# Four stacked graph layers on one core: how the edge keys are made, which branch body comes first, and where the last turned copies stand

## Time and profile before

| | |
|---|---|
| median of 3 runs | 1550.4 us (1550.18 to 1551.41) |
| the profiled execution | 1550.59 us |
| its span, first to last instruction | 1548.6 us |
| TensorE (PE) busy | 1516.2 us, 98% |
| VectorE (DVE) busy | 881.2 us, 57% |
| ScalarE (ACT) busy | 751.6 us, 49% |
| GpSimd (POOL) busy | 189.9 us, 12% |
| mean granted TensorE clock | 0.997 |
| bytes by DMA | 231.88 MB, mean 150 GB/s |

### The profile page before, as it was taken

How to read it: one execution, slowest core, us unless ns; L and a number is a source line. 1 busy time by engine, 2 the same in 40 slices (tenths; PEclk the granted TensorE clock), 3 DMA queues, 4 the chain that set the end, 5 groups by cost and what they waited for, 6 DMA issues and landing times.

```text
span 1548.6 us, 19194 instructions
## 1 busy us (share of the span) xinstructions
PE 1516.2 (98%) x6956; PEld 1218.0 (79%) x6956; DVE 881.2 (57%) x1403; ACT 751.6 (49%) x1358; POOL 189.9 (12%) x315
## 2 busy tenths in 40 slices
PE   5989999999999999999999999999999999999997
PEld 4877877778887887788877777888888778877775
DVE  7877888887736343322433244567598356434346
ACT  5666766767734333333332234345597236533232
POOL 1101021234300000000000000112143013100003
PEclk9999999999999999999999999999999999999999
DMA  5333143324774433434353424564466248535345
GB/s 175 121 110 132 42 167 128 112 75 158 253 259 174 132 136 112 166 106 138 100 172 125 156 68 145 189 233 168 143 184 194 87 149 294 189 129 171 93 126 179
DMA packets 103328, 231.88 MB, mean 150 GB/s; under 512 B 23167, under 2 KB 26102, under 8 KB 103226
## 3 DMA queue, kind: packets, MB, share of 16 engines
q1 hardware_dynamic: 90126, 191.66, 38.8%
q10 hardware_dynamic: 13100, 38.86, 6.5%
HBM read 171.11 MB, written 59.37 MB: 149 GB/s over the span
## 4 chain that ended last, share of the span: by engine, by line
PE 90%; DVE 5%; ACT 3%; issue 1%; DMA 0%; POOL 0%; DVEq 0%; SPq 0%; POOLq 0%; ACTq 0%
PE bank L974 16%; PE bank L836 15%; PE bank L838 15%; PE bank L837 15%; PE bank L985 9%; PE bank L978 7%; PE bank L976 7%; PE bank L1038 2%; ACT Tt L1119 2%; PE bank L906 1%; DVE Tt L1423 1%; PE bank L874 1%; DVE oK L1698 1%; ACT Mh L1101 0%; ACT Zh L1153 0%
## 5 line engine op out<-in xcount | busy, mean ns | idle before, releaser
L836 PE MATMUL bank<-wh,xh 128*125 128x512 f32 x1032 | 415.9, 403 | 0.0
L837 PE MATMUL bank<-wl,xh 128*125 128x512 f32 x1040 | 410.8, 395 | 0.0
L838 PE MATMUL bank<-wh,xl 128*125 128x512 f32 x1040 | 410.0, 394 | 0.0
L974 PE MATMUL bank<-Zh,Mh 125*125 125x512 f32 x1000 | 399.4, 399 | 0.0
L1397 DVE TENSOR_TENSOR xl<-xs,xh 128x1000 fp32r<-128x1000 f32 x130 | 155.5, 1198 | 291.6 <-ACT xh L1084 291.3
L1084 ACT CAST xh<-xs 128x1000 fp32r<-128x1000 f32 x130 | 132.9, 1026 | 304.2 <-PE bank L838 292.8
L985 PE MATMUL bank<-Zl,Mh 125*125 125x512 f32 x600 | 236.6, 394 | 0.0
L838 PEld LDWEIGHTS bank<-wh,xl 128*125 128x125 f32 x1040 | 193.3, 186 | 49.0
L837 PEld LDWEIGHTS bank<-wl,xh 128*125 128x125 f32 x1040 | 193.4, 186 | 44.5
L836 PEld LDWEIGHTS bank<-wh,xh 128*125 128x125 f32 x1032 | 191.4, 185 | 44.6
L974 PEld LDWEIGHTS bank<-Zh,Mh 125*125 125x125 f32 x1000 | 185.4, 185 | 44.7
(11 more groups left out here) (173 smaller groups left out, 1812.2 us busy)
## 6 DMA issues: line engine op xcount, KB each, us to landing
xs<-xT_d SPq DMA_DIRECT2D x80, 500.0 KB, 3.5
Ar<-a_d SPq DMA_DIRECT2D x100, 312.5 KB, 3.3
xs<-hT_d SPq DMA_DIRECT2D x40, 500.0 KB, 3.5
x_d<-XO ACTq DMA_DIRECT2D x30, 512.0 KB, 5.1
R<-x_d SPq DMA_DIRECT2D x60, 256.0 KB, 4.3
xT_d<-XT ACTq DMA_DIRECT2D x30, 500.0 KB, 3.8
ws<-in_W SPq DMA_DIRECT2D x30, 256.0 KB, 3.6
Tt<-m_d SPq DMA_DIRECT2D x10, 625.0 KB, 5.0
```

Of the source, the lines that this page charges most:

```text
L836: te.matmul(o, xh[i % 2][:, k, :], wh[s][:], start=(k == 0), stop=False)
L837: te.matmul(o, xh[i % 2][:, k, :], wl[s][:], start=False, stop=False)
L838: m = te.matmul(o, xl[i % 2][:, k, :], wh[s][:], start=False, stop=(k == 7))
L974: te.matmul(o, Mh[i][:, s, :], zh, start=(n == 0), stop=False)
```

## The change

- `WIN` becomes 37 nodes for every chunk, centred on round((125 c + 62) / 17), no longer clipped. The table `win` and its load go. The centre `mid` is made on the chip from `iot`, which now starts at -180 (`ZERO` = 180 is where its value is 0).
- `ef`, `wt` and the two comparisons go. `off` = dst - mid is taken straight from the integers; one instruction takes the largest square of it, and the flag compares that with 18 squared. hi is rounded in two steps instead of three, lo16 is made in one step, kb = 10 off + hi. The general body makes `lo` and `key` for itself.
- TensorE's branch is written out: the counting body comes first, then the general one. The counting body ends with a jump over the general body. A hint for this jump is marked 30 chunks ahead.
- The whole copy into `A16` is a function of its own, `counts_whole`. For t = 9 it runs after counts_turned(9) and the first tanh, which now comes after counts_turned(9). VectorE runs degrees(5, 10) before times.

```diff
-MARGIN = 250
+REACH = 18
+HINT = 30
+ZERO = NT * REACH
+WHOLE = 12582912.0
-WIN = [(max(0, (T * c - MARGIN) // PER), min(N - 1, (T * c + T - 1 + MARGIN) // PER)) for c in range(NC)]
+WIN = [(round((T * c + T // 2) / PER) - REACH, round((T * c + T // 2) / PER) + REACH) for c in range(NC)]
...
-            sy.dma_start(wn_[:], win.rearrange("p (a c) -> p a c", a=3)).then_inc(d_edge, 16)
...
-                with te.If(v > 0):
+                te.br_cond(v < 1, on_true="pe_chunks", on_false="pe_general")
+                with nc.body("pe_chunks", valid_engines=[te.engine]):
+                    for c in range(NC):
+                        if c == NC - HINT:
+                            hint = te.mark_branch_hint_location()
+                        chunk(c)
...
+                    te.br("pe_counted").branch_hint(hint)
+                after, q.seen = q.seen, before
+                with nc.body("pe_general", valid_engines=[te.engine]):
                     te.sem_inc(gP, 1)
...
+                    te.br("pe_counted")
+                nc.switch_bb("pe_counted")
...
+                if t < NT - 1:
+                    counts_whole(t)
+
+            def counts_whole(t):
+                q.wait_ge(s_ev, 3 * t + 3)
                 if t >= 2:
                     q.wait_ge(d_a[t % 2], 16 * (t // 2))
-                q.wait_ge(s_ev, 3 * t + 3)
                 q.wait_ge(s_pad, 2)
                 ac.copy(A16[t % 2], Af[t % 2][:]).then_inc(s_a16, 1)
...
-                if t == NT - 1:
-                    tanh(J0[0], blocks_of(J0[0], EARLY))
                 counts_turned(t)
...
+            tanh(J0[0], blocks_of(J0[0], EARLY))
+            counts_whole(NT - 1)
             first_part(J0[0], EARLY)
...
-                q.wait_ge(d_edge, 48)
-                chain("v", ve.tensor_copy(ef[:], ei[:]))
-                mine()
-                chain("v", ve.tensor_tensor(wt[:, 0, :], wn_[:, 0, :], ef[:, 1, :], ALU.subtract))
-                chain("v", ve.tensor_tensor(wt[:, 1, :], ef[:, 1, :], wn_[:, 1, :], ALU.subtract))
-                mine()
-                chain("v", ve.reduce_max(sm[0:T, 0:1], wt[:].rearrange("p a c -> p (a c)"), AXX))
-                mine()
-                ve.tensor_scalar(sm[0:T, 1:2], sm[0:T, 0:1], 0.0, None, ALU.is_gt).then_inc(s_flag, 1)
+                q.wait_ge(s_pool0, 1)
+                chain("v", ve.tensor_scalar(mid[:], iot[:, ZERO:ZERO + NC], float(T) / PER, float(T // 2) / PER, ALU.mult,
+                                            ALU.add))
+                mine()
+                chain("v", ve.tensor_scalar(mid[:], mid[:], WHOLE, -WHOLE, ALU.add, ALU.add))
+                mine()
+                q.wait_ge(d_edge, 32)
+                chain("v", ve.tensor_tensor(off[:], ei[:, 1, :], mid[:], ALU.subtract))
+                mine()
+                chain("v", ve.tensor_tensor_reduce(out=key[:], in0=off[:], in1=off[:], scale=1.0, scalar=0.0, op0=ALU.mult,
+                                                   op1=ALU.max, accum_out=sm[0:T, 0:1]))
+                mine()
+                ve.tensor_scalar(sm[0:T, 1:2], sm[0:T, 0:1], REACH * REACH + 0.5, None, ALU.is_gt).then_inc(s_flag, 1)
...
-                chain("v", ve.scalar_tensor_tensor(lo[:], hi[:], -float(T), ef[:, 0, :], ALU.mult, ALU.add))
-                chain("v", ve.scalar_tensor_tensor(key[:], ef[:, 1, :], float(NT), hi[:], ALU.mult, ALU.add))
-                mine()
-                chain("v", ve.tensor_copy(lo16[:], lo[:].unsqueeze(2).to_broadcast([T, NC, 2])))
-                chain("v", ve.tensor_tensor(kb[:], key[:], wn_[:, 2, :], ALU.subtract))
-                mine()
-                q.wait_ge(s_pool0, 1)
+                chain("v", ve.scalar_tensor_tensor(lo16[:], hi[:].unsqueeze(2).to_broadcast([T, NC, 2]), -float(T),
+                                                   ei[:, 0, :].unsqueeze(2).to_broadcast([T, NC, 2]), ALU.mult, ALU.add))
+                chain("v", ve.scalar_tensor_tensor(kb[:], off[:], float(NT), hi[:], ALU.mult, ALU.add))
+                mine()
...
-                times(J0[0], EARLY)
                 degrees(5, NT)
+                times(J0[0], EARLY)
```

More of the change, by code:

```diff
@@ L364, with gnn_program @@
 STORE = {j: i for i, j in enumerate(STORES)}
-def gnn_program(nc, xT, x, es, ed, win, W1, b1, gw, gb, Ws0, Wn0, b0, Ws1, Wn1, bb1, W2, a2, W3, b3, out):
+def gnn_program(nc, xT, x, es, ed, W1, b1, gw, gb, Ws0, Wn0, b0, Ws1, Wn1, bb1, W2, a2, W3, b3, out):
     f32, fr, bf, f16 = mybir.dt.float32, mybir.dt.float32r, mybir.dt.bfloat16, mybir.dt.float16
@@ L450, in gnn_program @@
         ei = sb("ei", [T, 2, NC], i32, ca)
[L451 to L454, removed]
+        mid, off, hi, lo, key, kb = (sb(n, [T, NC], f32, ca) for n in ("mid", "off", "hi", "lo", "key", "kb"))
         lo16 = sb("lo16", [T, NC, 2], f16, ca)
@@ L513, in gnn_program @@
         s_row, s_q, s_pu = (sem(n) for n in ("s_row", "s_q", "s_pu"))
+        s_whole = sem("s_whole")
         s_own = {n: sem(f"s_own_{n}") for n in ("v", "a", "p")}
@@ L918, in build @@
                 before = dict(q.seen)
-                with te.If(v > 0):
+                te.br_cond(v < 1, on_true="pe_chunks", on_false="pe_general")
[4 more added lines that the diff above has]
+                        chunk(c)
+                        if c in X0_AT:
+                            x0_upper(X0_AT.index(c))
+                        for u in range(X_UNITS):
+                            if X_AT[u] == c:
+                                x_part(u // 8, u % 8, u >= 8)
+                        for b in range(NT - 1):
+                            for n in range(3):
+                                if c == C_LAST[3 * b + 2] + 4 + 2 * n:
+                                    at_part(b, n)
+                        if c == C_LAST[3 * NT - 4] + 10:
+                            first_rows()
+                    te.br("pe_counted").branch_hint(hint)
+                after, q.seen = q.seen, before
+                with nc.body("pe_general", valid_engines=[te.engine]):
                     te.sem_inc(gP, 1)
@@ L1653, in prologue @@
                 ve.memset(zz[:], 0.0).then_inc(s_zz, 1)
-                q.wait_ge(d_edge, 48)
-                chain("v", ve.tensor_copy(ef[:], ei[:]))
+                q.wait_ge(s_pool0, 1)
+                chain("v", ve.tensor_scalar(mid[:], iot[:, ZERO:ZERO + NC], float(T) / PER, float(T // 2) / PER, ALU.mult,
+                                            ALU.add))
                 mine()
-                chain("v", ve.tensor_tensor(wt[:, 0, :], wn_[:, 0, :], ef[:, 1, :], ALU.subtract))
-                chain("v", ve.tensor_tensor(wt[:, 1, :], ef[:, 1, :], wn_[:, 1, :], ALU.subtract))
+                chain("v", ve.tensor_scalar(mid[:], mid[:], WHOLE, -WHOLE, ALU.add, ALU.add))
                 mine()
-                chain("v", ve.reduce_max(sm[0:T, 0:1], wt[:].rearrange("p a c -> p (a c)"), AXX))
+                q.wait_ge(d_edge, 32)
+                chain("v", ve.tensor_tensor(off[:], ei[:, 1, :], mid[:], ALU.subtract))
                 mine()
-                ve.tensor_scalar(sm[0:T, 1:2], sm[0:T, 0:1], 0.0, None, ALU.is_gt).then_inc(s_flag, 1)
-                chain("v", ve.tensor_scalar(hi[:], ef[:, 0, :], 1.0 / T, -62.0 / T, ALU.mult, ALU.add))
+                chain("v", ve.tensor_tensor_reduce(out=key[:], in0=off[:], in1=off[:], scale=1.0, scalar=0.0, op0=ALU.mult,
+                                                   op1=ALU.max, accum_out=sm[0:T, 0:1]))
                 mine()
-                chain("v", ve.tensor_scalar(lo[:], hi[:], 12582912.0, None, ALU.add))
+                ve.tensor_scalar(sm[0:T, 1:2], sm[0:T, 0:1], REACH * REACH + 0.5, None, ALU.is_gt).then_inc(s_flag, 1)
+                chain("v", ve.tensor_scalar(hi[:], ei[:, 0, :], 1.0 / T, -62.0 / T, ALU.mult, ALU.add))
                 mine()
-                chain("v", ve.tensor_scalar(hi[:], lo[:], -12582912.0, None, ALU.add))
+                chain("v", ve.tensor_scalar(hi[:], hi[:], WHOLE, -WHOLE, ALU.add, ALU.add))
                 mine()
@@ L1689, in low_part @@
                                  lo16[:, BATCH * i:BATCH * (i + 1), :].unsqueeze(2).to_broadcast([T, BATCH, PAIRS, 2]),
-                                 iot[:, 0:2 * PAIRS].rearrange("p (l k) -> p l k", k=2).unsqueeze(1)
+                                 iot[:, ZERO:ZERO + 2 * PAIRS].rearrange("p (l k) -> p l k", k=2).unsqueeze(1)
                                  .to_broadcast([T, BATCH, PAIRS, 2]), ALU.is_equal).then_inc(s_ol, 1)
@@ L1727, in build @@
                     q.wait_ge(s_ok, HEAD)
+                    ve.scalar_tensor_tensor(lo[:], hi[:], -float(T), ei[:, 0, :], ALU.mult, ALU.add).then_inc(s_whole, 1)
+                    ve.scalar_tensor_tensor(key[:], ei[:, 1, :], float(NT), hi[:], ALU.mult, ALU.add).then_inc(s_whole, 1)
+                    ve.wait_ge(s_whole, 2)
                     for g in range(8):
@@ L1736, in build @@
                                 ve.sem_clear(gP)
```

(10 more changed lines are left out.)

1 line of the change is left out of this document (removed).

## The result

| | before | changed |
|---|---|---|
| median | 1551.59 us (1550.18 to 1552.10, 6 runs) | 1544.82 us (1543.31 to 1545.37, 6 runs) |
| span of the profiled execution | 1548.6 us | 1541.5 us |
| mean granted clock | 0.997 | 0.998 |

The ratio is 0.9957 (95% interval 0.9947 to 0.9968): 6.7 us less, between 5.0 and 8.2. The forecast was 7.6 less. The time alone doesn't tell the forecast (1543.0) from the first rival (1545.8): 1544.82 lies between them. The traces do.

What follows compares the result with a forecast made beforehand. TensorE, busy 98% of the span, was taken as the bound, so only its holes could be won: 5.9 (start) + 1.7 (end of counting) + 0 = 7.6, 1550.6 - 7.6 = 1543.0 us, range 1540.9 to 1546.4.

Steps and rivals of the forecast that it cites:

- the first rival: TensorE's jump after counting: the hint doesn't work, 2.8 us exposed, time 1545.8 us; chance 20%.
- (a) to (c): VectorE's prologue: edges land at an estimated 4.9, steps sum to 2.96 us against 5.24.
- (d): VectorE's flag or first hi step waits for GpSimd's memset until 6.79; first key at 9.1 instead of 7.9.
- (e): Start of counting: chunk 0 at 9.4, key 8 at 10.96 instead of 16.84; 5.9 us won.
- (f): Counting windows: nine more matmuls, 2% fewer columns; taken at 0 (bounds -0.5 and 0.8).
- (g): TensorE's jump at the end of counting: hinted 30 chunks ahead, 0; unhinted, 2.8 us exposed (bounds 0 and 3.5).
- (h): Before TensorE's last transposes: hole of 2.72 becomes 0.3, 2.4 us won, plus 1.4 of half clock.
- (i): Second gate product: x1_post(9) starts 1.7 us earlier; end of counting wins 1.7 (bounds 0.2 and 2.4).
- (j): SP's stores after counting: last at_d store held to 118.2, some 2 us cover it before ScalarE's wait; 0.
- The start's stall stays: Start: chunk body's code still fetched behind bulk loads, key 8 at 16.84, only 1.7 won, 1548.9 us; chance 7%.
- slower: TensorE's branches: each costs a fetch, the old one stays and a new one is added, 1553.8 us; chance 4%.

Runs made afterwards that it cites:

- hi_stt: Changed kernel with the two rounding steps of hi written as scalar_tensor_tensor instead of tensor_scalar; 1544.07 us, ratio to before 0.9955.
- no_hint: Changed kernel without the hint for the jump at the end of the counting body; 1547.00 us, ratio to before 0.9972.
- hint_near: Changed kernel with the hint marked 5 chunks before the jump instead of 30; 1544.18 us (one run).
- the second trace: Changed kernel run once more without any edit; 1545.17 us, ratio to before 0.9955.
- best: Changed kernel with hi by scalar_tensor_tensor, general body first and its jump hinted at TensorE's start, upper Z parts before second early tanh; 1545.77 us, ratio 0.9970.
- old_tail: Changed kernel with the order of the last copies, the first tanh and the degrees as before; 1544.30 us, ratio to before 0.9958.
- branch_only: Kernel before with only TensorE's new layout of the two bodies and the hint; 1546.93 us, ratio to before 0.9973.
- quiet_fetch: Changed kernel with TensorE's test laid out as before and SyncE's bulk loads held until VectorE has written four keys; 1547.76 us (one run).

## Why the prediction was right

- **(a) to (c), the shorter prologue.** Edges land at 5.13 (4.9 estimated), `off` 0.34, the maximum 0.38 to the next start, lo16 0.42, as priced; kb 0.28 to the next start instead of 0.30. First key at 8.90, forecast 9.1. That the edges landed 0.2 later than estimated cost nothing only because the brake of (d) held longer.
- **(d), the brake.** Right, and it was worth a term: in the changed kernel's two traces the edges land at 5.13 and 5.30 and hi's first step ends at 7.00 in both. `hi_stt` shows both the cause and the price (0.64 at equal landing of the edges; the forecast's difference was 1.2, as it held the flag too and the edges came earlier in it). The flag, one element wide, wasn't held: it ran from 5.88 to 6.03 beside the memset. That is most of why the start is 0.25 better than forecast.
- **(e), the start.** 5.9 forecast, 6.15 measured; first matmul at 9.36 (9.4). ScalarE's slabs stayed hidden. In `hi_stt`, 0.7 us earlier, TensorE waits 0.6 for them, without loss at gate 2.
- **(f), the windows.** The page has nine matmuls more (6965 against 6956), as counted. Taken at 0; from the start to 95.62 the lead fell by 0.08.
- **(g), the jump.** This is the term that was mis-sized: taken at 0 when hinted, it measured 0.65 and 1.0 in the changed kernel's two traces and 0.54 to 1.0 in seven. The first rival's premise didn't come true, but its price did nearly: 2.5 instead of 2.8 exposed, and then 1.56 for the clock (130.16 - 128.60, `no_hint` against `hint_near`), which I had not charged to it.
- **(h), (i), the tail.** The hole went from 2.72 to 0.33 (0.3), the first gate product gained 9.12 - 5.42 = 3.7 over x_part(8) (3.8), the second 7.22 - 5.42 = 1.80 (1.7). TensorE's waits for Mh and Ml are 0.96 and 0.77 (1.0 and 0.7). The order of lateness was as written: second tanh, upper Z, lower Z, x1_post(9). The bound of 0.2, "if these waits bring the half clock again", was no idle one: it came in the second trace, at a price of 1.4.
- **(j).** The last at_d store went out at 112.66, 4.25 ahead of before; GpSimd waited for it until 116.09, and ScalarE had 2 us to spare.
- **The rivals.** "The start's stall stays" and "slower" fell: no q8 packet lands before 20 us in the changed kernel.
- **Sum.** 5.9 + 1.7 - 0 was forecast, 6.15 + 1.80 - 0.73 measured (the last is the jump and 0.08 of drift before it): 7.2 at gate 2, 7.1 in the span, 6.8 in the medians. Errors of both signs partly cancel in it (+0.25, +0.1, -0.73). Of the 1.8 us between 1543.0 and 1544.82 about 1.0 is the kernel before, whose median over six runs is 1551.59, where the forecast started from 1550.6. The lower end of the range was added up with 2.1 for the tail, though (i) gives 2.4. My reading of the earlier trace rows was right in that the hole was a jump's fetch slowed by bulk loads; their end is not what set the landing (`best`: 11.0, with the DMA engines still full).

## What to carry to other kernels

Lay out the body that runs as the one that falls through, above all at a kernel's start, where bulk loads slow the fetch that a jump needs; if the jump must be somewhere, mark its hint early, away from such loads (16 us ahead worked here, 2.5 us did not, nothing between was tried), and put it in front of a wait that is there anyway. Price an edit in the company of the others: here 0.24 and 3.97 made 6.15, and the jump cost nothing under the old tail and 0.65 under the new one. Before reading a difference of 1 or 2 us between two kernels, run one of them twice and look for where the clock fell. When a hole of TensorE closes, follow the next engine's line to the product that waits for it: of 3.7 us won at the first gate product 1.8 arrived at the second, and the waits that ate the rest can cost the clock.

## What was not expected of the hardware

- A hint as the first instruction, some 7 us ahead of the jump and into saturated loads, bought 0.16 us; 5 chunks (about 2.5 us) ahead in a quiet stretch it bought 0.24; 30 and 100 chunks ahead bought 1.5 to 2.0. The first two are within what one program varies.
- In all jumps at the start, work begins 2.5 to 3.3 us after the packet of instructions has landed. In `quiet_fetch` these are 2.6 of the 4.5 us, so more than half of a quiet jump is not the transfer.
- The clock fell to half behind holes of 1.89 (`old_tail`), 2.29 and 2.72 us, and stayed full behind holes of 2.05 (`hint_near`), 1.74 (`branch_only`) and, near the start, 2.48 (`quiet_fetch`). Behind two waits of 0.95 and 0.77 us, 1.5 us apart, it fell in one trace of the changed kernel and not in the other. So in these traces the length of the hole alone doesn't decide it, and the program alone doesn't either.
